# Rotary attention loop of a four-layer kernel: from sixteen steps of 128 queries to eight key chunks of 256 queries

## The chip, the cores and the metric

The kernel runs on one core of a Trainium2 chip, as one program. The time is the device time of one execution in microseconds (us). A core has these engines: PE (TensorE, matrix multiplies; its weight loads are listed apart as PEld), DVE (VectorE), ACT (ScalarE), POOL (GpSimd) and SP (SyncE, which here only issues DMAs). Each engine runs its own instructions in order and waits on semaphores that others raise. Matrix results land in PSUM, which has eight banks of 128 x 512 fp32; everything else is in SBUF.

## The reference

The input `x` is 8 images of 32 x 32 tokens with 192 channels, fp32. Four layers follow one another, each of the form `x = x + layer(_gn(x))` with a group normalisation without weights. Layers 0 and 2 are attention with relative positions, layer 1 is windowed attention with registers. Layer 3, which the change touches, is this, cut to what matters (12 heads of 16 channels):

```python
q = x @ wq.T + bq;  k = (x @ wk.T + bk) * scaling;  v = x @ wv.T + bv
qr = theta_shift(qh, sin, cos);  kr = theta_shift(kh, sin, cos)    # rotary
qk = einsum('bnld,bnmd->bnlm', qr, kr) + mask                      # mask: (12, 1024, 1024)
out = einsum('bnlm,bnmd->bnld', softmax(qk, axis=-1), vr)
return (out + lepe(v)) @ wo.T + bo
```

For each image and head there are 1024 x 1024 scores, a full mask of the same size is added, and the softmax runs over the 1024 keys.

## The kernel before, in words

`program` runs the layers in turn. For layer 3, `prepare_rot` writes the rotated queries and keys and the values to DRAM, and `attend_rot` does the attention. All of the change is in `attend_rot`.

`attend_rot` works through 96 units: 3 groups of 4 heads, times 4 quarters of the queries (256 each), times 8 images. A unit has 256 queries, seen as two blocks of 128 (index `c`), 4 heads (`G`; in two pairs `p`, two sides `sd`), and 1024 keys in 8 chunks of 128 (`kc`). One unit goes through these stages:

- `scores` (PE, L2413), four calls per unit, one for each (c, p): four matmuls of 512 columns fill `S`, which takes four PSUM banks and is one buffer. A call therefore waits (`s_done`) until DVE has read the result of the call before.
- `row_max` (DVE): for each of the two heads of a call a pass (L2498) adds the mask, writes the sum to `X` in SBUF and keeps the row maximum. Then DVE subtracts the maximum for one of the two heads (L2503, "scalar" below), and ACT does so for the other (`lower`, L2550). They raise `x_dve` and `x_act`.
- `transposed` (PE, L2426): four 128 x 128 transposes of `X` fill one bank of `T`. `T` is a ring of three banks, taken in the order of `ORDER`: the transposes, and the two steps of the tail. `free` makes each wait for the reader of what stood three places before.
- `exponential` (ACT, L2531): the exponential of one bank of `T`, 128 x 512, into `PROB`, a ring of four in SBUF.
- `outputs` (PE, L2438): values times `PROB`, accumulated in `O` over the key chunks. The four heads are four column strips of 32. It has eight matmul instructions (two per head, as the trace counts them) of 128 columns.
- The tail of a unit runs inside the next one: ACT copies `O` to `OSB` (L2539); PE spreads the softmax sums (`turn`, L2449, two matmuls of 256 columns); DVE takes the reciprocal (L2509) and multiplies (L2511), together `divide`; PE projects (`wo`, L2454, four matmuls of 256 columns); ACT copies to `Y` (L2544); POOL adds it to the output in DRAM.

The order of PE's work is written out by hand. `body(u)` has 16 steps; step s is block c = s // 8, chunk kc = s % 8. A step does `transposed(s)`, a `scores` call of the next unit in chunks 1 and 5 of either block, `outputs(s - 1)`, and after steps 3 and 6 the tail's `turn` and `wo`. The transposes of block 0 wait for the four rows of block 0 alone, those of block 1 for block 1. ACT's order is written beside it: the exponentials, `lower` after steps 1, 5, 9 and 13 (that of the pair (1, 1) in step 1 of the unit that uses it), the two copies after steps 0 and 6. DVE does `row_max(0, 0)`, `divide`, `row_max(0, 1)`, `(1, 0)`, `(1, 1)`. PE and ACT run two units per turn of a hardware loop (`Fori`). Before each group of PE instructions stands `alone(pe)`, a nop that carries the waits.

Of the kernel before, what the change touches and what calls it, by code (L numbers as in the profile page):

```python
# [42 lines left out]
def need(eng, sem, value, solo=False):  # L43

    if isinstance(value, int) and value <= 0:
        return
    eng.wait_ge(sem, value)
    if solo:
        alone(eng)
# [2190 lines left out]
def attend_rot(nc, sems, name, stream, w, ident, part_rows, v_rows):  # L2240

    QUARTERS = GROUPS * 4
    UNITS = QUARTERS * IMAGES
    RING, PRING = 3, 4
    STEPS = 2 * CHUNKS
    SCORES_AT = {1: 0, 5: 1}
    TAIL = ("turn", "wo")
    TAIL_AT = {3: "turn", 6: "wo"}
    ORDER = [n for s in range(STEPS) for n in [("t", s)] + ([TAIL_AT[s]] if s in TAIL_AT else [])]
    assert len(ORDER) % RING == 0  # L2250

    def kind(n):
# [10 lines left out]
    def slot(n):  # L2263
        return ORDER.index(n) % RING

    with ExitStack() as ctx:
        def sb(n, shape, dt=F32):
            return ctx.enter_context(nc.sbuf_tensor(f"{name}_{n}", shape, dt))
# [12 lines left out]
        K = sb("K", [P, 2, 2, TOKENS], F32R)  # L2281
        QR = sb("QR", [P, 2, 2, 2 * P], F32R)
        V = sb("V", [P, 2, CHUNKS, G, 2 * DIM])
        PROB = sb("PROB", [P, PRING, G, P])
        OSB = sb("OSB", [P, 2 * P])
        inverse = sb("inverse", [P, 2 * P])
        Y = sb("Y", [HALF, 2, 2, 2 * P])
# [102 lines left out]
        def _(pe):  # L2390
# [24 lines left out]
                        if kh:  # L2415
                            last.then_inc(s_ready, 1)

            def transposed(u, par, s):
                c, kc = divmod(s, CHUNKS)
                free(u, ("t", s))  # L2420
                if kc == 0:
                    pe.wait_ge(x_dve, G * u + 2 * (c + 1))
                    pe.wait_ge(x_act, G * u + 2 * (c + 1))
                alone(pe)
                for g in range(G):
                    last = nc.tensor.transpose(T[:, slot(("t", s)), P * g:P * g + P], X[:, par, c, g, P * kc:P * kc + P],  # L2426
                                               ident_sb[:])
                last.then_inc(t_ready, 1)

            def outputs(u, par, s, mine=None):  # L2430
                c, kc = divmod(s, CHUNKS)
                pe.wait_ge(t_act, upto(u, ("t", s), "act"))
                if s == 0:
                    pe.wait_ge(v_loaded[par], V_LOADS * mine)
                    need(pe, o_out, u)
                alone(pe)
                for g in range(G):
                    last = nc.tensor.matmul(O[Q * g:Q * g + Q, par, P * c:P * c + P], V[:, par, kc, g],  # L2438
                                            PROB[:, s % PRING, g], start=kc == 0, stop=kc == CHUNKS - 1)
                last.then_inc(pv_done, 1)  # L2440

            def tail(u, par, n):
# [20 lines left out]

            def body(u, par, mine, nth):

                for s in range(STEPS):
                    c, kc = divmod(s, CHUNKS)
                    transposed(u, par, s)
                    if kc in SCORES_AT and not (isinstance(u, int) and u == UNITS - 1):
                        scores(u + 1, 1 - par, c, SCORES_AT[kc], nth)  # L2470
                    if s:
                        outputs(u, par, s - 1, mine)
                    elif not isinstance(u, int) or u:
                        outputs(u - 1, 1 - par, STEPS - 1)
                    if s in TAIL_AT and (not isinstance(u, int) or u):
                        tail(u, par, TAIL_AT[s])

            def epilogue():
                outputs(UNITS - 1, 1, STEPS - 1)
                for n in TAIL:  # L2480
                    tail(UNITS, 0, n)

# [4 lines left out]
        def _(eng):  # L2487
# [26 lines left out]
                for p in range(2):  # L2514
                    row_max(0, c, p)
            for u in range(UNITS + 1):
                for c in range(2):
                    if u + 1 < UNITS:
                        row_max(u + 1, c, 0)
                    if c == 0 and u:  # L2520
                        divide(u - 1)
                    if u + 1 < UNITS:
                        row_max(u + 1, c, 1)


        @block.scalar
        def _(act):
            def exponential(u, s):
                act.wait_ge(t_ready, upto(u, ("t", s), "pe"))
                need(act, pv_done, STEPS * u + s - PRING + 1, solo=True)  # L2530
                nc.scalar.activation(PROB[:, s % PRING].rearrange("p g x -> p (g x)"), T[:, slot(("t", s))], ACT.Exp,  # L2531
                                     scale=-1.0).then_inc(t_act, 1)

            def outputs(u, opar):
                act.wait_ge(pv_done, STEPS * u)
                if not isinstance(u, int) or u > 1:
                    act.wait_ge(t_ready, upto(u - 1, "wo", "pe"))
                alone(act)
                nc.scalar.copy(OSB[:], O[:, opar]).then_inc(o_out, 1)  # L2539

            def projected(u, ypar, stores):
                act.wait_ge(t_ready, upto(u, "wo", "pe"))
                need(act, y_stored[ypar], 16 * stores, solo=True)
                nc.scalar.copy(Y[:, ypar].rearrange("p m t -> p (m t)"), T[0:HALF, slot("wo")]).then_inc(t_act, 1)  # L2544

            def lower(v, par, c, p):

                act.wait_ge(s_done, TILES_U * v + G * c + 2 * p + 2)
                here = X[:, par, c, 2 * p + 1]
                nc.scalar.activation(here, here, ACT.Identity, scale=-1.0, bias=rmax[:, par, c, 2 * p + 1:2 * p + 2]  # L2550
                                     ).then_inc(x_act, 1)

            def body(u, par, stores):
                last = isinstance(u, int) and u == UNITS - 1
                for s in range(STEPS):
                    exponential(u, s)
                    c, kc = divmod(s, CHUNKS)
                    if kc == 1 and c == 0:
                        lower(u, par, 1, 1)
                    elif kc == 1 and not last:  # L2560
                        lower(u + 1, 1 - par, 0, 1)
                    if kc == 5 and not last:
                        lower(u + 1, 1 - par, c, 0)
                    if not isinstance(u, int) or u:
                        if s == 0:
                            outputs(u, 1 - par)
                        if s == 6:
                            projected(u, 1 - par, stores)

            for c, p in ((0, 0), (0, 1), (1, 0)):  # L2570
                lower(0, 0, c, p)
            for u in range(4):
                body(u, u % 2, (u - 1) // 2)
            with act.Fori(2, UNITS // 2 - 1) as p:
                body(2 * p, 0, p - 1)
                body(2 * p + 1, 1, p)
            body(UNITS - 2, 0, UNITS // 2 - 2)
            body(UNITS - 1, 1, UNITS // 2 - 1)
            outputs(UNITS, 1)
            projected(UNITS, 1, UNITS // 2 - 1)  # L2580

# [137 lines left out]
```

## Time and profile before

| what | value |
|---|---|
| time, median of 3 runs | 9231.04 us (9228.94 to 9237.27) |
| time of the profiled execution | 9223.04 us |
| its span, first to last instruction | 9221.4 us |
| the loop of `attend_rot`, first to last exponential | 7320.5 to 9208.5 us of the span |
| PE busy over the span | 7542.9 us (82%) |
| DVE, ACT, POOL busy | 57%, 49%, 28% |
| granted PE clock, mean | 0.900 of full speed |

The span is measured from the first to the last instruction of the profiled execution; the 1.6 us around it are start and end. A busy share is an average over four layers with different limits, so the rows further down are of stretches of the rotary loop. A granted clock of 1.00 is 2.4 GHz and 0.50 is 1.2 GHz. A timeline row gives when a run of like instructions starts, how long it takes from its first start to its last end, and in brackets how long the engine had been idle and what ended that.

### The profile page before, as it was taken

The numbers are of one execution on the slowest core, as the hardware profiler recorded it, in microseconds if no ns is written. First come the engines' busy times: TensorE is split into PE (matmuls) and PEld (weight loads), VectorE is DVE, ScalarE is ACT, GpSimd is POOL, SyncE is SP. The second block draws the span as 40 slices with busy tenths as digits, with TensorE's granted clock in tenths as the row PEclk, the third lists the DMA queues.
The fourth block names the chain that finished last, engine by engine and source line by source line (L and its number), as shares of the span: only waits on it lengthen the run. The fifth ranks groups of instructions, "written<-read, shape, count | busy, mean of one in ns | idle before, by whom it ended". The sixth has DMA issues, their size and how long they took to land. (4 is left out here: it accounts for less than half of the span.)

```text
span 9221.4 us, 201937 instructions
## 1 busy us (share of the span) xinstructions
PE 7542.9 (82%) x68440; PEld 4564.9 (50%) x68440; DVE 5284.4 (57%) x7803; ACT 4527.8 (49%) x8209; POOL 2587.1 (28%) x2843
## 2 busy tenths in 40 slices
PE   2988889889388878846889888888576699999999
PEld 2555555555155555524555555554232355555555
DVE  3555555555255555544555555554677477777776
ACT  1444444444265655632444444445233377777776
POOL 2343434333021121114433333342455300000000
PEclk7899999999698999977999998999677799999999
DMA  6666666665433333346665665664221344444443
GB/s 160 130 119 135 122 130 118 130 123 105 112 70 68 75 70 71 74 118 126 126 128 120 122 126 118 123 117 74 92 72 62 88 123 112 126 111 123 115 122 82
DMA packets 536710, 999.89 MB, mean 108 GB/s; under 512 B 102129, under 2 KB 303026, under 8 KB 500210
## 3 DMA queue, kind: packets, MB, share of 16 engines
q1 hardware_dynamic: 479346, 900.57, 43.6%
q0 software_dynamic: 56576, 88.90, 6.2%
q8 instruction: 485, 7.95, 0.4%
q14 instruction: 303, 2.48, 0.1%
HBM read 646.02 MB, written 335.81 MB: 106 GB/s over the span
## 5 line engine op out<-in xcount | busy, mean ns | idle before, releaser
L1676 DVE TENSOR_REDUCE a_nmp<-a_S 128x2 f32<-128x1024 f32 x1536 | 1878.3, 1224 | 1433.6 <-PE a_S L1524 1430.5
L1777 ACT ACTIVATE a_PROB<-a_T 128x512 f32<-128x512 f32 x3072 | 1667.3, 595 | 1977.5 <-PE a_T L1503 1964.2
L1373 POOL CAST a_RF<-a_RL 32x512 fp32r<-32x512 f32 x1536 | 1295.2, 843 | 1011.8 <-DVE a_RL L1704 919.9
L2498 DVE CUSTOM_DVE_ANT_0 a_X<-a_S,a_mask 128x1024 f32<-128x1024 f32 x768 | 909.3, 1221 | 608.7 <-PE a_S L2413 593.4
L2531 ACT ACTIVATE a_PROB<-a_T 128x512 f32<-128x512 f32 x1536 | 918.2, 598 | 439.1 <-PE a_T L2426 429.3
L1499 PE MATMUL a_T<-a_QW,a_KW 64*128 64x512 f32 x3072 | 801.1, 514 | 402.0 <-issue 149.1
L2426 PE MATMUL a_T<-a_ident,a_X 128*128 128x128 f32 x6144 | 994.6, 285 | 32.2 <-DVE a_OSB L2511 16.5
L1499 PEld LDWEIGHTS a_T<-a_QW,a_KW 64*128 64x128 f32 x3072 | 311.3, 191 | 1427.1 <-issue 1424.2
L1537 PE MATMUL a_O<-a_PROB,a_V 128*32 128x512 f32 x6144 | 887.8, 652 | 2.9 <-ACT a_PROB L1777 2.5
L962 DVE CUSTOM_DVE_ANT_0 a_PROB<-a_S,a_mask 128x512 f32<-128x512 f32 x768 | 522.9, 688 | 598.5 <-PE a_PT L799 505.8
L2426 PEld LDWEIGHTS a_T<-a_ident,a_X 128*128 128x128 f32 x6144 | 660.0, 141 | 327.1 <-issue 305.5
L1524 PEld LDWEIGHTS a_S<-a_KV,a_QV 64*128 64x128 f32 x6144 | 652.1, 199 | 116.8
L1518 PE MATMUL a_S<-a_KW,a_QW 64*128 64x512 f32 x3072 | 662.8, 418 | 27.3 <-DVE a_nmp L1676 27.3
L1503 PE MATMUL a_T<-a_QV,a_KV 64*128 64x512 f32 x3072 | 648.0, 409 | 35.1 <-issue 35.1
L1524 PE MATMUL a_S<-a_KV,a_QV 64*128 64x256 f32 x6144 | 660.9, 290 | 0.0
L2438 PE MATMUL a_O<-a_PROB,a_V 128*32 128x128 f32 x12288 | 655.0, 284 | 2.0 <-ACT a_PROB L2531 0.5
L2369 POOL DMA_DIRECT2D out<-a_Y x96 | 92.0, 959 | 1845.6 <-ACT a_PROB L2531 1832.5
L1043 ACT ACTIVATE a_PROB<-a_PROB,a_nmax 128x512 f32<-128x512 f32 x768 | 550.4, 719 | 76.1 <-DVE a_nmax L962 76.1
L1564 PE MATMUL a_T<-a_QC,a_tab_d 16*32 16x64 f32 x6144 | 414.3, 300 | 181.9 <-issue 106.0
L799 PE MATMUL a_PT<-a_ident,a_PROB 128*128 128x128 f32 x3072 | 491.8, 285 | 50.4 <-ACT a_PROB L1043 31.0
L1564 PEld LDWEIGHTS a_T<-a_QC,a_tab_d 16*32 16x32 f32 x6144 | 362.8, 127 | 207.8 <-issue 186.5
L2550 ACT ACTIVATE a_X<-a_X,a_rmax 128x1024 f32<-128x1024 f32 x384 | 438.6, 1142 | 38.0 <-DVE a_rmax L2498 38.0
(160 smaller groups left out, 10640.8 us busy)
## 6 DMA issues: line engine op xcount, KB each, us to landing
a_QV<-a_part_rows SPq DMA_DIRECT2D x384, 256.0 KB, 7.1
a_rel_rows<-a_RF SPq DMA_DIRECT2D x96, 1024.0 KB, 9.2
a_K<-part_rows SPq DMA_DIRECT2D x576, 128.0 KB, 3.3
a_X<-xn_scratch SPq DMA_DIRECT2D x72, 768.0 KB, 6.4
stream<-a_Y POOLq DMA_DIRECT2D x288, 192.0 KB, 5.7
a_part_rows<-a_part SPq DMA_DIRECT2D x48, 1024.0 KB, 11.8
a_QV<-a_part_rows SPq DMA_DIRECT2D x384, 128.0 KB, 7.7
a_QV<-a_rel_rows SPq DMA_DIRECT2D x384, 128.0 KB, 7.4
```

Of the source, the lines that this page charges most:

```text
L1373: nc.gpsimd.tensor_copy(dst, src).then_inc(permuted, 1)
L1499: nc.tensor.matmul(T[:, slot(("st", s, pr, sd))], KW[lines, keys], QW[lines, par, pr, cols], start=True, stop=False)
L1518: nc.tensor.matmul(S[:, pr, sd], QW[lines, par, pr, queries], KW[lines, kh * BANK:(kh + 1) * BANK], start=True, stop=False)
L1524: last = nc.tensor.matmul(S[:, pr, sd, here], QV[lines, par, pr, 2 * kh + kq, queries], KV[lines, par, pr, keys], start=False, stop=kq == 1)
L1537: last = nc.tensor.matmul(O[Q * g:Q * g + Q], V[:, par, kc, g], PROB[:, s % PRING, g], start=kc == 0, stop=kc == CHUNKS - 1)
L1564: last = nc.tensor.matmul(T[at + 32:at + 64, to, 64 * a:64 * a + 64], tab_d[:, x], QC[:, :, half * BANK + x:(half + 1) * BANK:SIDE], start ...
L1676: nc.vector.tensor_reduce(nmp[:, qh, c, 2 * pr:2 * pr + 2, kh], S[:, pr], AX.X, ALU.max).then_inc(s_done, 1)
L1777: nc.scalar.activation(PROB[:, s % PRING, 2 * pr + sd], T[:, slot(("st", s, pr, sd))], ACT.Exp).then_inc(t_act, 1)
L2426: last = nc.tensor.transpose(T[:, slot(("t", s)), P * g:P * g + P], X[:, par, c, g, P * kc:P * kc + P], ident_sb[:])
L2438: last = nc.tensor.matmul(O[Q * g:Q * g + Q, par, P * c:P * c + P], V[:, par, kc, g], PROB[:, s % PRING, g], start=kc == 0, stop=kc == CHU ...
L2498: nc.vector.tensor_tensor_reduce(out=X[:, v % 2, c, g], in0=S[:, sd].rearrange("p a b -> p (a b)"), in1=mask[:, n % 2, g, c], scale=1.0, s ...
L2531: nc.scalar.activation(PROB[:, s % PRING].rearrange("p g x -> p (g x)"), T[:, slot(("t", s))], ACT.Exp, scale=-1.0).then_inc(t_act, 1)
```

## The change: steps over key chunks

The unit keeps its 256 queries, 4 heads and 8 key chunks. `body` now has 8 steps, one for each key chunk.

- In a step PE fills two banks of `T` one after the other: `transposed(kc, 0)` has the heads of pair 0 for both query blocks, `transposed(kc, 1)` those of pair 1. There are 16 such calls per unit as before, of four transposes each. The first of a unit waits for all eight rows of the unit (both blocks and pairs) where it waited for four.
- ACT takes the exponential of each bank; the two fill one entry of `PROB`, which is twice as wide (256 queries). The ring has three entries and not four.
- `outputs` runs once per key chunk, 8 times per unit and not 16, with eight matmul instructions of 256 columns each.
- The four `scores` calls of the next unit stand in steps 0, 2, 3 and 5. In sixteenths of the unit they stood at 1, 5, 9 and 13; now they stand at 0, 4, 6 and 10.
- The tail: `turn` after step 1, `wo` after step 4 (sixteenths 2 and 8; they stood at 3 and 6).
- ACT's `lower` calls for the next unit stand in steps 2, 4, 5 and 7. The last, for the pair (1, 1), stands behind the last exponential of the unit; it stood in the second step of the unit that uses it. The prologue lowers four pairs and not three.
- DVE's order of calls is the same. SP's and POOL's programs are not touched.

The diff, with PE's `body` and `tail` order, ACT and DVE:

```diff
@@ -2241,12 +2241,12 @@
 
     QUARTERS = GROUPS * 4
     UNITS = QUARTERS * IMAGES
-    RING, PRING = 3, 4
-    STEPS = 2 * CHUNKS
-    SCORES_AT = {1: 0, 5: 1}
+    RING, PRING = 3, 3
+    SCORES_AT = {0: (0, 0), 2: (0, 1), 3: (1, 0), 5: (1, 1)}
     TAIL = ("turn", "wo")
-    TAIL_AT = {3: "turn", 6: "wo"}
-    ORDER = [n for s in range(STEPS) for n in [("t", s)] + ([TAIL_AT[s]] if s in TAIL_AT else [])]
+    TAIL_AT = {1: "turn", 4: "wo"}
+    LOWER_AT = {2: (0, 0), 4: (0, 1), 5: (1, 0), 7: (1, 1)}
+    ORDER = [n for s in range(CHUNKS) for n in [("t", s, 0), ("t", s, 1)] + ([TAIL_AT[s]] if s in TAIL_AT else [])]
     assert len(ORDER) % RING == 0
 
     def kind(n):
@@ -2281,7 +2281,7 @@
         K = sb("K", [P, 2, 2, TOKENS], F32R)
         QR = sb("QR", [P, 2, 2, 2 * P], F32R)
         V = sb("V", [P, 2, CHUNKS, G, 2 * DIM])
-        PROB = sb("PROB", [P, PRING, G, P])
+        PROB = sb("PROB", [P, PRING, G, 2 * P])
         OSB = sb("OSB", [P, 2 * P])
         inverse = sb("inverse", [P, 2 * P])
         Y = sb("Y", [HALF, 2, 2, 2 * P])
@@ -2415,28 +2415,27 @@
                         if kh:
                             last.then_inc(s_ready, 1)
 
-            def transposed(u, par, s):
-                c, kc = divmod(s, CHUNKS)
-                free(u, ("t", s))
+            def transposed(u, par, kc, p):
+                free(u, ("t", kc, p))
+                if kc == 0 and p == 0:
+                    pe.wait_ge(x_dve, G * (u + 1))
+                    pe.wait_ge(x_act, G * (u + 1))
+                alone(pe)
+                for sd in range(2):
+                    for c in range(2):
+                        last = nc.tensor.transpose(T[:, slot(("t", kc, p)), P * (2 * sd + c):P * (2 * sd + c) + P],
+                                                   X[:, par, c, 2 * p + sd, P * kc:P * kc + P], ident_sb[:])
+                last.then_inc(t_ready, 1)
+
+            def outputs(u, par, kc, mine=None):
+                pe.wait_ge(t_act, upto(u, ("t", kc, 1), "act"))
                 if kc == 0:
-                    pe.wait_ge(x_dve, G * u + 2 * (c + 1))
-                    pe.wait_ge(x_act, G * u + 2 * (c + 1))
-                alone(pe)
-                for g in range(G):
-                    last = nc.tensor.transpose(T[:, slot(("t", s)), P * g:P * g + P], X[:, par, c, g, P * kc:P * kc + P],
-                                               ident_sb[:])
-                last.then_inc(t_ready, 1)
-
-            def outputs(u, par, s, mine=None):
-                c, kc = divmod(s, CHUNKS)
-                pe.wait_ge(t_act, upto(u, ("t", s), "act"))
-                if s == 0:
                     pe.wait_ge(v_loaded[par], V_LOADS * mine)
                     need(pe, o_out, u)
                 alone(pe)
                 for g in range(G):
-                    last = nc.tensor.matmul(O[Q * g:Q * g + Q, par, P * c:P * c + P], V[:, par, kc, g],
-                                            PROB[:, s % PRING, g], start=kc == 0, stop=kc == CHUNKS - 1)
+                    last = nc.tensor.matmul(O[Q * g:Q * g + Q, par], V[:, par, kc, g], PROB[:, kc % PRING, g],
+                                            start=kc == 0, stop=kc == CHUNKS - 1)
                 last.then_inc(pv_done, 1)
 
             def tail(u, par, n):
@@ -2463,20 +2462,20 @@
 
             def body(u, par, mine, nth):
 
-                for s in range(STEPS):
-                    c, kc = divmod(s, CHUNKS)
-                    transposed(u, par, s)
+                for kc in range(CHUNKS):
+                    for p in range(2):
+                        transposed(u, par, kc, p)
                     if kc in SCORES_AT and not (isinstance(u, int) and u == UNITS - 1):
-                        scores(u + 1, 1 - par, c, SCORES_AT[kc], nth)
-                    if s:
-                        outputs(u, par, s - 1, mine)
+                        scores(u + 1, 1 - par, *SCORES_AT[kc], nth)
+                    if kc:
+                        outputs(u, par, kc - 1, mine)
                     elif not isinstance(u, int) or u:
-                        outputs(u - 1, 1 - par, STEPS - 1)
-                    if s in TAIL_AT and (not isinstance(u, int) or u):
-                        tail(u, par, TAIL_AT[s])
+                        outputs(u - 1, 1 - par, CHUNKS - 1)
+                    if kc in TAIL_AT and (not isinstance(u, int) or u):
+                        tail(u, par, TAIL_AT[kc])
 
             def epilogue():
-                outputs(UNITS - 1, 1, STEPS - 1)
+                outputs(UNITS - 1, 1, CHUNKS - 1)
                 for n in TAIL:
                     tail(UNITS, 0, n)
 
@@ -2514,25 +2513,27 @@
                 for p in range(2):
                     row_max(0, c, p)
             for u in range(UNITS + 1):
-                for c in range(2):
-                    if u + 1 < UNITS:
-                        row_max(u + 1, c, 0)
-                    if c == 0 and u:
-                        divide(u - 1)
-                    if u + 1 < UNITS:
-                        row_max(u + 1, c, 1)
+                if u + 1 < UNITS:
+                    row_max(u + 1, 0, 0)
+                if u:
+                    divide(u - 1)
+                if u + 1 < UNITS:
+                    row_max(u + 1, 0, 1)
+                    row_max(u + 1, 1, 0)
+                    row_max(u + 1, 1, 1)
 
 
         @block.scalar
         def _(act):
-            def exponential(u, s):
-                act.wait_ge(t_ready, upto(u, ("t", s), "pe"))
-                need(act, pv_done, STEPS * u + s - PRING + 1, solo=True)
-                nc.scalar.activation(PROB[:, s % PRING].rearrange("p g x -> p (g x)"), T[:, slot(("t", s))], ACT.Exp,
-                                     scale=-1.0).then_inc(t_act, 1)
+            def exponential(u, kc, p):
+                act.wait_ge(t_ready, upto(u, ("t", kc, p), "pe"))
+                if p == 0:
+                    need(act, pv_done, CHUNKS * u + kc - PRING + 1, solo=True)
+                nc.scalar.activation(PROB[:, kc % PRING, 2 * p:2 * p + 2].rearrange("p g x -> p (g x)"),
+                                     T[:, slot(("t", kc, p))], ACT.Exp, scale=-1.0).then_inc(t_act, 1)
 
             def outputs(u, opar):
-                act.wait_ge(pv_done, STEPS * u)
+                act.wait_ge(pv_done, CHUNKS * u)
                 if not isinstance(u, int) or u > 1:
                     act.wait_ge(t_ready, upto(u - 1, "wo", "pe"))
                 alone(act)
@@ -2552,22 +2553,18 @@
 
             def body(u, par, stores):
                 last = isinstance(u, int) and u == UNITS - 1
-                for s in range(STEPS):
-                    exponential(u, s)
-                    c, kc = divmod(s, CHUNKS)
-                    if kc == 1 and c == 0:
-                        lower(u, par, 1, 1)
-                    elif kc == 1 and not last:
-                        lower(u + 1, 1 - par, 0, 1)
-                    if kc == 5 and not last:
-                        lower(u + 1, 1 - par, c, 0)
-                    if not isinstance(u, int) or u:
-                        if s == 0:
-                            outputs(u, 1 - par)
-                        if s == 6:
-                            projected(u, 1 - par, stores)
-
-            for c, p in ((0, 0), (0, 1), (1, 0)):
+                later = not isinstance(u, int) or u
+                for kc in range(CHUNKS):
+                    exponential(u, kc, 0)
+                    exponential(u, kc, 1)
+                    if kc == 0 and later:
+                        outputs(u, 1 - par)
+                    if kc in LOWER_AT and not last:
+                        lower(u + 1, 1 - par, *LOWER_AT[kc])
+                    if kc == 4 and later:
+                        projected(u, 1 - par, stores)
+
+            for c, p in ((0, 0), (0, 1), (1, 0), (1, 1)):
                 lower(0, 0, c, p)
             for u in range(4):
                 body(u, u % 2, (u - 1) // 2)
```

## Rows read from the trace of the kernel before

**Rows 1.** Busy time in 300 us of the loop: PE, PEld, DVE, ACT, POOL, clock, DMA.
```profile
7700.00:8000.00 300.00, 294.15 (x3252) 175.78 (x3245) 216.68 (x335) 218.36 (x334) 14.38 (x15) 1.00 0.43 115
```

**Rows 2.** DMA issues from 7700 to 8900 us: count, KB each, median us to landing.
```profile
a_V<-v_rows SPq DMA_DIRECT2D x61, 512.0 KB, 4.2
```

**Rows 3.** The tile a_PROB, its exponentials: shortest/median/longest ns, first and last start.
```profile
L2531 ACT ACTIVATE a_PROB<-a_T x1536: 588/597/602, 7320.5 to 9208.5; 128x512 f32<-128x512 f32 x192
```

**Rows 4.** Timeline of PE: start, length, line, operation, count, idle before.
```profile
8029.62 0.63 PE L2426 MATMUL a_T<-a_ident,a_X 128*128 128x128 f32 x4 [0.29 <-issue]
...
8034.06 0.70 PE L2449 MATMUL a_T<-a_OSB,a_turn 128*128 128x256 f32 x2
8034.60 0.60 PE L2426 MATMUL a_T<-a_ident,a_X 128*128 128x128 f32 x4
8035.13 0.43 PE L2438 MATMUL a_O<-a_PROB,a_V 128*32 128x128 f32 x8
8035.48 0.66 PE L2426 MATMUL a_T<-a_ident,a_X 128*128 128x128 f32 x4
8036.07 0.73 PE L2413 MATMUL a_S<-a_K,a_QR 48*128 48x512 f32 x4
8036.73 0.42 PE L2438 MATMUL a_O<-a_PROB,a_V 128*32 128x128 f32 x8
8037.34 0.63 PE L2426 MATMUL a_T<-a_ident,a_X 128*128 128x128 f32 x4 [0.18 <-DVE a_OSB L2511]
...
8038.25 1.10 PE L2454 MATMUL a_T<-a_OSB,a_wo 128*96 128x256 f32 x4
8039.19 0.60 PE L2426 MATMUL a_T<-a_ident,a_X 128*128 128x128 f32 x4
8039.73 0.42 PE L2438 MATMUL a_O<-a_PROB,a_V 128*32 128x128 f32 x8
```

**Rows 5.** Timeline in layer 0: an output group of 512 columns and what follows.
```profile
2008.89 1.07 PE L1537 MATMUL a_O<-a_PROB,a_V 128*32 128x512 f32 x8
...
2009.89 0.50 PE L1499 MATMUL a_T<-a_QW,a_KW 64*128 64x512 f32 x2
```

**Rows 6.** Timeline of all engines in one unit of the loop.
```profile
8006.21 0.42 PEld L2426 LDWEIGHTS a_T<-a_ident,a_X 128*128 128x128 f32 x4 [0.20 <-issue]
...
8006.80 0.73 PE L2413 MATMUL a_S<-a_K,a_QR 48*128 48x512 f32 x4
8007.04 0.60 ACT L2531 ACTIVATE a_PROB<-a_T 128x512 f32<-128x512 f32 x1 [0.34 <-PE a_T L2426]
...
8007.53 1.14 ACT L2550 ACTIVATE a_X<-a_X,a_rmax 128x1024 f32<-128x1024 f32 x1
...
8007.70 1.23 DVE L2498 CUSTOM_DVE_ANT_0 a_X<-a_S,a_mask 128x1024 f32<-128x1024 f32 x1 [1.43 <-PE a_S L2413]
...
8014.47 0.75 DVE L2503 TENSOR_SCALAR a_X<-a_X,a_rmax 128x1024 f32<-128x1024 f32 x1
...
8015.13 1.75 DVE L2509 RECIPROCAL a_inverse<-a_T 128x256 f32<-128x256 f32 x1
...
8016.92 0.42 DVE L2511 TENSOR_TENSOR a_OSB<-a_OSB,a_inverse 128x256 f32<-128x256 f32 x1
...
8017.26 1.22 DVE L2498 CUSTOM_DVE_ANT_0 a_X<-a_S,a_mask 128x1024 f32<-128x1024 f32 x1
8017.46 0.42 PEld L2426 LDWEIGHTS a_T<-a_ident,a_X 128*128 128x128 f32 x4 [0.42 <-issue]
```

**Rows 7.** Timeline of the prologue, where `scores` has nothing else to wait for.
```profile
7307.93 1.23 DVE L2498 CUSTOM_DVE_ANT_0 a_X<-a_S,a_mask 128x1024 f32<-128x1024 f32 x1 [84.78 <-PE a_S L2413]
...
7310.22 0.75 DVE L2503 TENSOR_SCALAR a_X<-a_X,a_rmax 128x1024 f32<-128x1024 f32 x1
...
7310.42 0.53 PEld L2413 LDWEIGHTS a_S<-a_K,a_QR 48*128 48x128 f32 x4 [3.32 <-issue]
```

**Rows 8.** Busy time in a stretch of layer 1, columns as in Rows 1.
```profile
3900.00:4000.00 100.00, 84.26 (x937) 56.84 (x930) 64.03 (x167) 69.75 (x171) 16.04 (x22) 0.95 0.30 58
```

## The prediction, made before the changed kernel ran

> **What bounds the kernel now.** I read the busy time of a stretch first. In the loop PE is busy 294 of 300 us at a granted clock of 1.00 (2.4 GHz), while DVE and ACT have 217 and 218 [rows 1]. So the loop ends when PE's list of instructions ends, and the other two follow. The brackets of the timeline say the same: ACT sits idle 0.34 us until the transposes are there, DVE 1.43 us until the scores are there [rows 6]. The exponentials of units 0 to 95 start between 7320.5 and 9208.5 us, so a unit takes 1888 / 95.94 = 19.68 us [rows 3]. In the timeline of PE the reader is to see start-to-start times: transposes to scores 0.59, output group to transposes 0.35, scores to output group 0.66 [rows 4].
>
> From these a unit of before is 16 x (0.59 + 0.36) + 4 x 0.66, plus 0.48 for `turn` and 0.90 for `wo`, which is 19.2 us. Two small waits come on top. The transposes after step 5 start 0.61 us after the output group instead of 0.36, because DVE's multiply holds their bank: 0.25 us. The loop branch costs 0.36 us in every second unit, so 0.18 (0.29 us of idle in its row). Sum 19.6 us, against 19.68 measured. This method is then good to 0.1 us per unit, and I use it for the new order.
>
> **The change part by part: PE's work.**
>
> Output groups. At 128 columns a group takes 0.36 us until the next starts [rows 4], at 512 columns 1.00 us [rows 5]. On a straight line 256 columns take 0.36 + 0.64 / 3 = 0.573 us. The eight of them are 4.58 us, where sixteen took 5.76. The ends of the range are 0.50 (half of the 512 group) and 0.66.
>
> Pairs of transposes. Two groups in a row with nothing between are not in the trace. The nearest rows are `turn` followed by transposes. From a `turn` of the same 0.43 us of columns to the transposes is 0.54 us, and from these to the output group 0.53 [rows 4]. I take 0.535 + 0.54 = 1.075 us for a pair, against 2 x 0.59 = 1.18 apart. The ends are 0.86 + 0.11 (no gap at all between the two) and 1.18.
>
> The work of a new unit is 8 x 1.075 + 8 x 0.573 + 4 x 0.66 + 0.48 + 0.90 = 17.2 us, 2.0 us less than before. If nothing else changed, a unit would take 17.2 to 17.3 us.
>
> **The waits that it adds.** The steps are now bunched, so I lay out one unit by start times on PE, from its first transposes at 0. These pieces are measured:
> - scores to DVE's first pass 0.90 (8006.80 to 8007.70); transposes to exponential 0.83 (8006.21 to 8007.04); an exponential followed by ACT's next instruction 0.49 (8007.04 to 8007.53); `lower` 1.14 long [rows 6];
> - DVE: scalar to reciprocal 0.66, reciprocal to multiply 1.79, multiply to next pass 0.34; the end of the multiply (8017.34) to PE's start 0.12 [rows 6];
> - first pass to scalar 2.29, and first pass to the next `scores` call, when that waits for DVE, 2.49 [rows 7].
>
> First wait, the single score buffer. The scores (0,0) start at 1.075, DVE's passes at 1.98, the scalar at 4.27. PE goes on: scores 0.66 and outputs 0.573 (2.31), a pair and outputs (3.96), `turn`, ready some 0.9 later. So DVE takes the reciprocal at 4.93, the multiply at 6.72, and the passes for (0,1) only at 7.06. The scores (1,0) can then start at 7.06 + 2.49 = 9.55. Meanwhile PE has `turn` (to 4.43), a pair (5.51), scores (0,1) (6.17) and outputs (6.74). The next transposes take the bank of `turn`, which is free at 6.72 + 0.42 + 0.12 = 7.26: 0.52 us of wait. Their pair ends at 8.34, and the scores (1,0), one chunk behind (0,1), wait 1.21 us. Before, a `scores` call came every four of sixteen steps, some 4.5 us apart, which covers DVE's 3.4 us; now (0,1) and (1,0) are 2.3 us apart in PE's order and DVE has `divide` in front. Everything of PE queues behind that call, and ACT runs dry with it.
>
> Second wait, the end of the unit. From 9.55: scores and outputs (10.78); chunk 4 with `wo` 2.55 (13.33); chunk 5 with scores 2.31 (15.64); chunk 6 1.65 (17.29). The last pair starts at 17.29. Its first exponential starts at 18.12, its second at 18.61, and only then comes `lower` (1,1), from 19.10 to 20.24. The next unit's first transposes need it: 20.24 + 0.12 = 20.36. PE had its last outputs of this unit done at 18.94, so it waits 1.42 us. The branch of 0.36 us lies inside this wait. Before, that same `lower` ran in step 1 and was needed in step 8. DVE's own part of these rows is done before (scores at 14.41, scalar at 17.6), so the wait is ACT's order and not its load.
>
> Sum of a unit: 17.2 + 0.52 + 1.21 + 1.42 = 20.36 us. That is 0.68 us more than 19.68: the 2.0 us of work and 0.43 of small waits come back, 3.15 of waits are added.
>
> **Parts at nothing.** `PROB` with three entries: the exponential of chunk kc needs the outputs of kc - 3, two chunks back in PE's order; if that cover went, ACT would wait, which has about a third of its time free. The copies to `OSB` and `Y`: ACT idles until the next exponential. SP: the load of V is issued after `wo`, now at about 13.4 of 20.4 us, and is needed at 3.4 of the next unit, so it has 10 us; it lands in 4.2 [rows 2]. The operands are loaded more than a unit ahead, as before. POOL only stores, a unit behind.
>
> **The ends.** Unit 0 waits for all four pairs of rows, some 4 us more than now (the first pass of the fourth pair plus 2.4 for DVE and 1.3 for `lower`). But it has no tail and no `divide` in its chain, which makes it about 1 us shorter than before, and the last unit has no scores: 8 x 1.65 = 13.2 against 16 x 0.95 = 15.2. Together about +1 us.
>
> 94 units x 0.68 + 1 = 65 us. The profiled execution of 9223 us (span 9221.4) becomes 9288. The median of the runs shown is 8 us above it, so I predict 9296 us.
>
> **A rule of the skill on the clock.** During the loop, where about half of PE's time is transposes, the granted clock is 1.00 [rows 1]. The Trainium skill, page "TensorE: Matmul & The Clock Gate", section "Part 4: PE-mode transpose", says that the full clock "doesn't engage" for transposes, as they do not count as busy in the same way. The trace does not agree as long as PE has no gaps. The changed loop has gaps, with pairs of transposes on both sides of them; that is the second rival.
>
> **The rivals.**
> - Cheap pairs: the second group of transposes streams right behind the first, and the output group is at its low end, 0.50. For it: after `turn` and `wo` the transposes' weights are loaded early (their own length is 0.60 and not 0.66) [rows 4]. Against: 0.54 us from `turn` to transposes is already 0.11 above bare streaming. With pairs at 0.97 and groups at 0.50 the same layout, laid out anew, gives 19.65 us per unit, as now: 9229. With cheap pairs alone it gives 19.94: 9231 + 94 x 0.26 + 1 = 9256. Chance 0.15, of which 0.09 for what lies within 18 us of before.
> - The clock falls: for a stretch after the gaps of 1.2 and 1.4 us PE runs at 1.2 GHz. For it: in layer 1, with PE busy 84 of 100 us, the mean clock is 0.95 [rows 8], and the changed loop has 17.2 / 20.36 = 84%. Against: 0.95 is still mostly full clock, and the instructions there are others. A mean of 0.95 is a tenth of the time at half clock, 2 us of each unit, in which half of the work comes late: 1.0 us per unit, 9296 + 94 = 9390. Chance 0.13.
> - No waits: DVE and ACT hand over in time and PE's work alone counts, 17.3 us per unit: 9231 - 94 x 2.4 = 9005. It would need the reciprocal and `lower` to be off the chain, and the rows put them on it. Chance 0.04.
>
> The other side decides at one point: when the sum of the three waits is under 2.4 us per unit, the change is faster.
>
> **How the numbers follow.** The forecast itself has 0.68; its own range, with pairs of 1.00 to 1.18 (20.1 to 20.8 us per unit), is 9268 to 9345. A measurement of this kernel can tell 0.2% (18 us) from no change. Faster by more than that is the no-wait case and the far end of the cheap pairs: 0.06. The same is their middle: 0.09. Slower is the rest: 0.85. For the range I go down to 9245, inside the cheap pairs, and up to 9385, almost the whole of the clock case.
>
> **What would show it.** In the trace after: output groups of 256 columns 0.57 us before their successor; the second transposes 0.54 us after the first; two idle times of PE per unit, over 1 us each, one before L2413 released by DVE L2498 in every unit, one before L2426 released by ACT L2550; a third of 0.5 us before L2426 released by DVE L2511; PE busy about 84% in the loop, clock 1.00; exponentials of a unit 20.4 us apart. The prediction is wrong if either long wait is missing, if pairs take under 1.0 us, or if the clock in the loop is under 0.98.

## The result: 0.8% slower, as forecast, by a sum whose parts were each somewhat off

The changed kernel takes 9297.48 us (median of 5 runs), the kernel before 9231.04. The ratio is 1.0077, 95% interval 1.0056 to 1.0098. The forecast was 9296. In a later set of four executions of the same changed kernel one took 20728 us at a mean granted clock of 0.57; it is left out of that set's ratio.

The profiled execution took 9314.65 us, 92 more than that of before. Not all of it is the change. The layers ahead are the same code and end a little earlier or later from run to run: the first `scores` call starts at 7306.61 us before and at 7321.68 after, and at 7300.57 in another profile of the same changed kernel. From that call to the last instruction it is 1914.8 us before and 1990.9 after. The change costs 76 us there; the medians of all runs differ by 66.

The busy time of the loop, the row that answers to [rows 1], with the same columns:

```profile
7700.00:8000.00 300.00, 253.57 (x2213) 154.95 (x2212) 205.31 (x320) 201.55 (x325) 14.39 (x15) 0.98 0.49 118
```

PE is busy 254 of 300 us (85%) where it had 294, and the granted clock is 0.98 where it was 1.00. No engine is full any more. The exponentials, which answer to [rows 3]:

```profile
L2532 ACT ACTIVATE a_PROB<-a_T x1536: 591/596/621, 7339.4 to 9298.9; 128x512 f32<-128x512 f32 x192
```

(9298.9 - 7339.4) / 95.94 = 20.42 us per unit; the forecast had 20.36, before it was 19.68. Now one unit on PE, the rows that answer to [rows 4]:

```profile
8014.73 1.07 PE L2426 MATMUL a_T<-a_ident,a_X 128*128 128x128 f32 x8 [1.39 <-issue]
8015.73 0.73 PE L2413 MATMUL a_S<-a_K,a_QR 48*128 48x512 f32 x4
8016.39 0.64 PE L2437 MATMUL a_O<-a_PROB,a_V 128*32 128x256 f32 x8
8016.96 1.09 PE L2426 MATMUL a_T<-a_ident,a_X 128*128 128x128 f32 x8
8017.98 0.64 PE L2437 MATMUL a_O<-a_PROB,a_V 128*32 128x256 f32 x8
8018.55 0.70 PE L2448 MATMUL a_T<-a_OSB,a_turn 128*128 128x256 f32 x2
8019.09 1.04 PE L2426 MATMUL a_T<-a_ident,a_X 128*128 128x128 f32 x8
8020.05 0.73 PE L2413 MATMUL a_S<-a_K,a_QR 48*128 48x512 f32 x4
8020.72 0.64 PE L2437 MATMUL a_O<-a_PROB,a_V 128*32 128x256 f32 x8
8021.95 1.06 PE L2426 MATMUL a_T<-a_ident,a_X 128*128 128x128 f32 x8 [0.59 <-DVE a_OSB L2510]
8024.23 0.73 PE L2413 MATMUL a_S<-a_K,a_QR 48*128 48x512 f32 x4 [1.22 <-DVE a_rmax L2497]
...
8032.81 0.64 PE L2437 MATMUL a_O<-a_PROB,a_V 128*32 128x256 f32 x8
8034.83 1.06 PE L2426 MATMUL a_T<-a_ident,a_X 128*128 128x128 f32 x8 [1.38 <-issue]
```

The reader is to see four things. The two groups of transposes of a step are now one run of eight and take 1.00 to 1.03 us to what follows, 0.96 behind `turn`. The output group takes 0.57. There are three idle times: 0.59 for the bank of `turn`, 1.22 in front of the scores (1, 0), and 1.4 in front of the next unit's first transposes. And the unit is 20.10 us long (8034.83 - 8014.73).

What ends the idle time of 1.4 us is shown as "issue"; the timeline of all engines at that place shows who holds PE back:

```profile
8012.51 1.08 ACT L2532 ACTIVATE a_PROB<-a_T 128x512 f32<-128x512 f32 x2 [0.50 <-PE a_T L2426]
...
8013.48 1.15 ACT L2551 ACTIVATE a_X<-a_X,a_rmax 128x1024 f32<-128x1024 f32 x1
8014.70 0.86 PEld L2426 LDWEIGHTS a_T<-a_ident,a_X 128*128 128x128 f32 x8 [1.84 <-issue]
```

Two exponentials, then `lower`, which ends at 14.63, and 0.07 us later PE loads weights. From 7700 to 8900 us these waits come once per unit (59 units; total, times, longest):

```profile
PE a_T L2426 <- issue: 81.7, 59, 1.4
PE a_S L2413 <- DVE a_rmax L2497: 70.9, 58, 1.2
...
PE a_T L2426 <- DVE a_OSB L2510: 34.4, 58, 0.9
```

The mean of a unit, 20.42 us, is above 20.10 because not all are alike. From reciprocal to reciprocal mostly three units take 20.1 us and the fourth 21.6 (23 such units in the loop). This is PE in a long one:

```profile
8042.05 1.06 PE L2426 MATMUL a_T<-a_ident,a_X 128*128 128x128 f32 x8 [0.59 <-DVE a_OSB L2510]
8044.33 1.04 PE L2413 MATMUL a_S<-a_K,a_QR 48*128 48x512 f32 x4 [1.22 <-DVE a_rmax L2497]
8045.31 1.08 PE L2437 MATMUL a_O<-a_PROB,a_V 128*32 128x256 f32 x8
8046.32 1.88 PE L2426 MATMUL a_T<-a_ident,a_X 128*128 128x128 f32 x8
8048.13 0.64 PE L2437 MATMUL a_O<-a_PROB,a_V 128*32 128x256 f32 x8
```

The busy time of 4 us around the same place, with the columns of [rows 1]:

```profile
8044.00:8048.00 4.00, 3.67 (x20) 2.12 (x20) 3.36 (x8) 0.40 (x1) 0.00 (x0) 0.57 0.01 2
```

Behind the idle times of 0.59 and 1.22 us the scores take 1.04 and not 0.73, the output group 1.08 and not 0.64, the transposes 1.88 and not 1.09. The granted clock of these 4 us is 0.57, so most of them ran at half clock (1.2 GHz); at 8048.13 all is at full length again. Such a stretch is called a dip from here on. From the scores to the output group at 8048.13 PE takes 3.80 us, where the unit before took 2.26 (8024.23 to 8026.49), and nothing behind takes the 1.54 us up: the unit is 1.55 us longer. 23 dips are 36 us. The remaining 40 us are 94 x (20.10 - 19.68); in that the prologue, 3.8 us longer, is about offset by the first and last units, which are shorter.

### The profile page after: what moved, and what is told of

It reads as the page before. It is cut to its first block and busy times, and to the rows that moved or that the text cites. A ratio compares the mean times of both kernels' runs of the same rounds, so it can differ in the third digit from the quotient of the medians.

```text
span 9312.6 us, 187162 instructions
## 1 busy us (share of the span) xinstructions
PE 7337.7 (79%) x62296; PEld 4460.8 (48%) x62296; DVE 5284.9 (57%) x7803; ACT 4460.1 (48%) x8209; POOL 2594.5 (28%) x2843
## 5 line engine op out<-in xcount | busy, mean ns | idle before, releaser
L1777 ACT ACTIVATE a_PROB<-a_T 128x512 f32<-128x512 f32 x3072 | 1667.9, 595 | 1962.4 <-PE a_T L1503 1949.5
L2532 ACT ACTIVATE a_PROB<-a_T 128x512 f32<-128x512 f32 x1536 | 835.8, 595 | 596.3 <-PE a_T L2426 589.3
L2426 PE MATMUL a_T<-a_ident,a_X 128*128 128x128 f32 x6144 | 842.4, 281 | 192.2 <-issue 127.2
L2426 PEld LDWEIGHTS a_T<-a_ident,a_X 128*128 128x128 f32 x6144 | 690.4, 144 | 470.0 <-issue 448.1
L2437 PE MATMUL a_O<-a_PROB,a_V 128*32 128x256 f32 x6144 | 501.4, 399 | 0.3 <-ACT a_PROB L2532 0.3
```

What stands on the lines that cost most here:

```text
L1777: nc.scalar.activation(PROB[:, s % PRING, 2 * pr + sd], T[:, slot(("st", s, pr, sd))], ACT.Exp).then_inc(t_act, 1)
L2426: last = nc.tensor.transpose(T[:, slot(("t", kc, p)), P * (2 * sd + c):P * (2 * sd + c) + P], X[:, par, c, 2 * p + sd, P * kc:P * kc + P], ...
L2437: last = nc.tensor.matmul(O[Q * g:Q * g + Q, par], V[:, par, kc, g], PROB[:, kc % PRING, g], start=kc == 0, stop=kc == CHUNKS - 1)
L2532: nc.scalar.activation(PROB[:, kc % PRING, 2 * p:2 * p + 2].rearrange("p g x -> p (g x)"), T[:, slot(("t", kc, p))], ACT.Exp, scale=-1.0). ...
```

## The experiments

Four kernels first, to see whether the two long waits are separate terms.

**Lowering of (1, 1) one step earlier.**

```diff
-    LOWER_AT = {2: (0, 0), 4: (0, 1), 5: (1, 0), 7: (1, 1)}
+    LOWER_AT = {2: (0, 0), 4: (0, 1), 5: (1, 0), 6: (1, 1)}
```

> The changed kernel with one edit: ACT lowers the pair (1, 1) after step 6 and not after step 7, so that it is done before the last exponentials of the unit. Theory A (the two long waits are separate terms, the one at the unit's end is ACT's order alone): the wait before the first transposes of a unit, 1.4 us, goes to about nothing; the loop branch of 0.36 us in every second unit shows again; the wait before the scores (1, 0) stays at 1.2. Undisturbed units of 18.8 and 19.2 us in turn instead of 20.10, time about 9190 with the clock's dips as they are. Theory B (the end wait only hides DVE's chain, the scores and row maxima are the real bound): the wait moves in front of a scores call and the unit stays within 0.2 us of 20.1. Theory C on the clock: the dips come at the scores wait, which stays, so the granted clock in the loop stays at 0.98 or so; if they need the end wait as well, it is 1.00.

Measured: 9257.65 us, ratio to before 1.0042 (1.0026 to 1.0057). The wait at the unit's end is gone, and a unit without a dip takes 18.89 us. But of the 95 steps from reciprocal to reciprocal only 18 are of that kind; 75 take 20.4 us or a little more. The busy time of 1200 us, with the clock of 0.93:

```profile
7700.00:8900.00 1200.00, 1087.46 (x8956) 653.57 (x8951) 845.82 (x1313) 816.75 (x1314) 57.31 (x60) 0.93 0.49 118
```

and PE around one dip, in a run of units of 20.45 us:

```profile
8014.86 1.06 PE L2426 MATMUL a_T<-a_ident,a_X 128*128 128x128 f32 x8 [0.59 <-DVE a_OSB L2510]
8017.15 0.73 PE L2413 MATMUL a_S<-a_K,a_QR 48*128 48x512 f32 x4 [1.22 <-DVE a_rmax L2497]
8017.81 1.08 PE L2437 MATMUL a_O<-a_PROB,a_V 128*32 128x256 f32 x8
8018.82 1.97 PE L2426 MATMUL a_T<-a_ident,a_X 128*128 128x128 f32 x8
```

The mechanism of theory A holds (18.89 against 18.8 and 19.2), theory B falls. The expectation of 9190 us missed by 68: the clock took back most of the 1.2 us per unit. Theory C expected a clock of 0.98 or 1.00, and it is 0.93. The units of 18.8 and 19.2 us in turn did not come either: the loop branch, 0.36 us in every second unit before the change, shows in none of the changed kernels whose wait at the unit's end is gone. Why is open.

**Scores (1, 0) in step 4.**

```diff
-    SCORES_AT = {0: (0, 0), 2: (0, 1), 3: (1, 0), 5: (1, 1)}
+    SCORES_AT = {0: (0, 0), 2: (0, 1), 4: (1, 0), 5: (1, 1)}
```

> The changed kernel with one edit: the scores (1, 0) are issued in step 4 and not in step 3. Theory A (single score buffer with the divide in DVE's chain): the wait of 1.2 us before scores (1, 0) goes, the 0.6 us before the transposes of step 3 stays, the wait at the unit's end stays at 1.4 us; units of 19.1 us instead of 20.10, time about 9200 before any effect of the clock. Theory B (DVE's chain is the bound): DVE's work only comes later, the unit's end waits longer by as much, and the unit stays at 20.1. Clock: with no wait over 0.6 us in mid-unit the dips in every fourth unit go and the clock in the loop is 1.00, which is worth another 0.39 us per unit, 37 us: 9165.

Measured: 9181.81 us, ratio 0.9956 (0.9940 to 0.9972). Units of 19.10 us throughout, no dips:

```profile
PE a_T L2426 <- issue: 87.2, 63, 1.4
...
PE a_T L2426 <- DVE a_OSB L2510: 37.3, 63, 0.9
...
PE a_S L2413 <- DVE a_rmax L2497: 13.6, 62, 0.2
```

The wait in front of the scores went from 1.2 to 0.2 us, and the one at the unit's end stayed at 1.4. So one digit in this table turns the change from slower into 0.4% faster. With idle times of 1.4, 0.6 and 0.2 us, each several us from the next, there is no dip here. The time is 17 us above the 9165 that was expected with the clock at 1.00.

**Both edits.**

> Both edits: scores (1, 0) in step 4, lowering of (1, 1) after step 6. Theory A: the gains add up, since each wait is a term of its own: units of 17.8 and 18.1 us in turn (PE's work of 16.9 us, 0.6 of wait for the divide, small waits, the branch), clock 1.00, time about 9055; faster than the kernel before the change by some 1.9%. Theory B: the second edit gains less than alone, because DVE's chain of four scores calls and one divide (4 x 3.4 + 2.1 = 15.7 us) is met; units over 18.5.

Measured: 9043.8 us, ratio 0.9813 (0.9792 to 0.9835), units of 17.86 us, clock 1.00. The two gains add up: 20.10 - 1.21 - 1.00 = 17.89. Theory B falls.

**Scores first.** Against the changed kernel, the call for (0, 0) moves ahead of the transposes of step 0, (1, 0) stands in step 4 as in the run before, and three lowerings come one step earlier:

```diff
-    SCORES_AT = {0: (0, 0), 2: (0, 1), 3: (1, 0), 5: (1, 1)}
-    LOWER_AT = {2: (0, 0), 4: (0, 1), 5: (1, 0), 7: (1, 1)}
+    SCORES_AT = {2: (0, 1), 4: (1, 0), 5: (1, 1)}
+    LOWER_AT = {1: (0, 0), 3: (0, 1), 5: (1, 0), 6: (1, 1)}
...
                 for kc in range(CHUNKS):
+                    if kc == 0 and not (isinstance(u, int) and u == UNITS - 1):
+                        scores(u + 1, 1 - par, 0, 0, nth)
                     for p in range(2):
                         transposed(u, par, kc, p)
```

> Scores (0, 0) of the next unit stand ahead of the first transposes, the others in steps 2, 4 and 5; lowering after steps 1, 3, 5 and 6. DVE starts its chain 1 us earlier in the unit. Theory A: the divide is then done before the transposes of step 3 want its bank, or nearly, and units take 17.5 and 17.8 us in turn, which is PE's work and the branch: time about 9030. Theory B: the scores call ahead of the transposes delays the first exponentials by 0.66 us and ACT's list becomes the bound; units above e3's.

Measured: 9008.1 us, ratio 0.9774 (0.9757 to 0.9790). Units of 17.38 us, PE busy 97% again:

```profile
7700.00:8000.00 300.00, 291.20 (x2590) 178.80 (x2589) 246.32 (x382) 232.72 (x379) 16.30 (x17) 1.00 0.55 134
```

This is the best version of the study, 2.3% faster than the kernel before the change. Theory B fell: the units are shorter than the 17.86 us of the kernel with both edits, and ACT is busy 233 of 300 us.

**Evenly spread scores.** The eight-chunk structure without the early scores:

```diff
-    SCORES_AT = {0: (0, 0), 2: (0, 1), 3: (1, 0), 5: (1, 1)}
+    SCORES_AT = {0: (0, 0), 2: (0, 1), 4: (1, 0), 6: (1, 1)}
```

> The changed kernel with the four scores calls evenly spread, in steps 0, 2, 4 and 6, as they were in sixteenths before; `lower` as in the change. So this is the eight-chunk structure without the early scores. Theory A (the early scores buy nothing, they cost): no wait in front of any scores call over 0.3 us, but the last one is later; ACT's order at the unit's end still costs 1.4 us; units of 19.1 us, clock 1.00, time within 15 us of the kernel with only scores (1, 0) moved (9182). Rival (the call in step 6 makes the row maximum of (1, 1) late for the unit's end): the chain scores 0.9, DVE 2.4, lower 1.3 from step 6 ends after ACT's last exponentials, and units are 19.6 or more.

Measured: 9209.4 us, ratio 0.9983 (0.9967 to 1.0000). Undisturbed units are 19.10 us, as expected. The wait at the unit's end is 1.67 us and follows ACT directly:

```profile
7761.18 1.06 PE L2426 MATMUL a_T<-a_ident,a_X 128*128 128x128 f32 x8 [1.67 <-ACT a_X L2551]
```

The time missed its expectation: it is 27 us above 9182, where 15 were allowed, because 29 of 95 units take 20.3 or 20.4 us, with a mean clock of 0.97 from 7700 to 8900 us. Behind the idle time of 1.67 us above, the transposes at 7763.72 us take 1.97 us where 1.09 is their length at full clock; the idle time before that, for the bank of `turn`, lies some 12 us earlier. So one idle time of 1.67 us can do what 1.4 did not. Why it does so in some units only, no run here shows.

**What brings the clock down.** Three kernels with useless work, all on the kernel with `lower` after step 6, where dips were most frequent. The transposes of step 3, pair 1, are issued three times:

```diff
             def transposed(u, par, kc, p):
...
                 alone(pe)
+                if (kc, p) == (3, 1):
+                    for _ in range(2):
+                        for sd in range(2):
+                            for c in range(2):
+                                nc.tensor.transpose(T[:, slot(("t", kc, p)), P * (2 * sd + c):P * (2 * sd + c) + P],
+                                                    X[:, par, c, 2 * p + sd, P * kc:P * kc + P], ident_sb[:])
```

> The kernel with `lower` (1, 1) after step 6, plus useless work: the four transposes of step 3, pair 1, are issued three times and not once (eight more transposes, 0.85 us), ahead of the wait for scores (1, 0). They lie inside that wait, so no chain gets longer. Theory C (the granted clock falls because PE is idle 0.6 and then 1.2 us of 2.9 us around that call): with 0.4 us of idle time left there the clock is 1.00, all units take 18.9 us where five of seven took 20.4, and the time falls by 94 x 1.1 = 100 us, to about 9155, although work was added. Rival D (transposes do not count for the clock, as the Trainium skill has it on its page TensorE: Matmul & The Clock Gate, Part 4): the dips stay, time about 9258. Rival E (the dips have another cause): the same.

In the second, ordinary matmuls stand in their place:

```diff
+                if (kc, p) == (3, 1):
+                    for sd in range(2):
+                        nc.tensor.matmul(T[:, slot(("t", kc, p)), 2 * P * sd:2 * P * sd + 2 * P], ident_sb[:],
+                                         X[:, par, sd, 2 * p, P * kc:P * kc + 2 * P], start=True, stop=True)
```

> As the run before, but the useless work is four ordinary fp32 matmul instructions of 256 columns (0.85 us) in front of the transposes of step 3, pair 1, written to the bank that these overwrite. Theory C: clock 1.00, units of 18.9 us, 9155. If D holds and transposes do not count but matmuls do, this one gets the clock back and the run before does not. Rival E: dips in both, 9258.

In the third, the condition is `(kc, p) == (2, 1)` and the transposes are issued twice:

> The kernel with `lower` (1, 1) after step 6, plus the transposes of step 2, pair 1, issued twice (0.43 us more), ahead of the wait of 0.6 us for the bank of `turn`. The wait of 1.2 us before scores (1, 0) stays. If both idle times together bring the clock down, dips become fewer or go: clock above 0.97, time 9160 to 9210. If the wait of 1.2 us is enough alone: clock 0.93 to 0.94, time about 9258.

Measured: 9152.17, 9151.44 and 9150.66 us, ratios 0.9926, 0.9918 and 0.9928 (lowest bound 0.9894, highest 0.9958). All three have units of 18.89 us throughout and a clock of 1.00; without the useless work it is 9257.65 us (ratio 1.0042). The undisturbed unit is the same 18.89 us with and without it, so the whole gain is the clock's. In the first, the idle times are 0.59 and 0.35 us, with 1.9 us of work between (8007.87 to 8009.81). The clock and the waits of the third, where only the first idle time was filled:

```profile
7700.00:8000.00 300.00, 276.39 (x2444) 170.93 (x2436) 225.24 (x350) 216.97 (x350) 15.34 (x16) 1.00 0.51 122
...
PE a_S L2413 <- DVE a_rmax L2503: 78.3, 64, 1.2
PE a_T L2432 <- DVE a_OSB L2516: 7.9, 48, 0.5
```

The wait of 1.2 us is still in every unit and does not bring the clock down alone. What did it was 0.59 and 1.22 us of idle time with one pair of transposes between. Filling either is enough. Rival D falls: transposes held the clock up as matmuls did. The Trainium skill, page "TensorE: Matmul & The Clock Gate", section "Part 4: PE-mode transpose", has it that transposes do not count as busy in the same way and that the full clock does not engage for them. These runs do not agree: 9152.17 us with transposes and 9151.44 with matmuls. Rival E falls with it.

**The changed kernel with the same fill, and the changed kernel again.** The first has the edit of the run with fill by transposes, on the changed kernel:

> The changed kernel itself with the useless transposes of step 3, pair 1 (issued three times), inside the wait for scores (1, 0). Theory C: the dips in every fourth unit go, all units take 20.10 us, clock in the loop 1.00; against the changed kernel 24 dips of 1.55 us fall away, 37 us, so the ratio to the kernel before is 1.0077 - 0.0040 = 1.0037 and the time some 9255. What then remains, 94 x (20.10 - 19.68) = 39 us, is the net of the change at full clock. Rival: the wait of 1.4 us at the unit's end keeps the dips, time unchanged at about 9290.

> The changed kernel as it is, on the same chip and beside the same runs of the kernel before as the run with fill. Every theory: ratio within 1.0056 to 1.0098, units of 20.1 us with one of 21.6 in every four, first exponential some microseconds earlier or later than in the profile before, as the layers ahead vary.

Measured, beside the same runs of before (median 9231.55 us): 9272.44 us, ratio 1.0040 (1.0027 to 1.0054), with the fill; ratio 1.0075 (1.0056 to 1.0095) without. With the fill the loop has units of 20.10 us throughout and this row:

```profile
8000.00:8300.00 300.00, 265.22 (x2361) 167.27 (x2361) 212.03 (x330) 204.56 (x329) 14.37 (x15) 1.00 0.49 118
```

The wait of 1.4 us at the unit's end is still there (83.0 us in 60 units), so it does not keep the dips. Of the 0.75 to 0.77% of the change, 0.40% is what the added waits cost beyond the saved work, at full clock, and some 0.35% is the clock.

## Why the prediction was right, step by step

- **PE's list bounds the loop before.** Right; where the waits are taken out, PE is 97% busy again (291 of 300 us) and the gain of the structure appears.
- **Output groups, 0.573 us.** Right: 0.57 from start to start (8006.38 to 8006.95 in the same profile). The straight line between 128 and 512 columns holds.
- **Pairs of transposes, 1.075 us.** Too high, and this was the largest error of the sum. They take 1.00 to 1.03 us, and 0.96 or 0.97 behind `turn` and `wo`. Together with the tail PE spends 9.5 us per unit on them, where the forecast had 9.98. The second group streams right behind the first. The lower end of the stated bounds (0.97) was nearer than the value taken. The work of a unit is 16.7 us and not 17.2.
- **First waits, 0.52 and 1.21 us.** Right in place and order. Against undisturbed start-to-start times (0.57 and 1.00) they are 0.66 and 1.28. PE came earlier, since its pairs were shorter, but DVE did not: the scores (1, 0) start 9.50 us into the unit (8014.73 to 8024.23), where the layout had 9.55.
- **Wait at the unit's end, 1.42 us.** Right: 1.45, and behind `lower` as forecast. The kernel with `lower` a step earlier loses it and 1.21 us per unit with it.
- **The sum of a unit, 20.36.** 16.7 + 3.4 = 20.10 at full clock. The excess of work (0.49) and the shortfall of the waits (0.25) partly cancelled: an error in PE's part in front of a wait for DVE is taken up by the wait. Behind the scores (1, 0) there is no such wait, and from there to the unit's end it is 10.60 us where the layout had 10.81.
- **The clock, a rival with chance 0.13.** It came, at a smaller size than priced: a mean of 0.98 and not 0.95, 0.39 us per unit and not 1.0. That 9296 lies so close to the measured time is luck: the clock, which the forecast's sum held at full speed, and the cheaper pairs cancel. By the forecast's own mechanism alone, with pairs as they were, the time would have been 9231 + 94 x 0.42 + 1 = 9271, and the run with fill measured 1.0040, which is 9268 for a kernel of 9231. That is slower too, but at the lowest end of the 9268 to 9345 that the prediction gives for its mechanism. The direction and the waits are earned, the last 25 us are not.
- **The line "clock under 0.98 in the loop" as a sign of error** was only just not met (0.98), and the sign "pairs under 1.0 us" was met by the two of eight pairs that stand behind `turn` and `wo`. Both point at the two terms that were off.
- **Parts at nothing.** Right: no wait on the load of V or on SP is among PE's waits in the loop. ACT waits there 357.2 us for the transposes and 34.7 us in front of the copy to `OSB`, and no wait for an entry of `PROB` is among its waits.
- **The loop branch.** The prediction places its 0.36 us inside the wait at the unit's end. Where that wait is gone it does not appear, so this part of the account is not borne out; it changed nothing in the sum.
- **The ends.** The prologue is longer as forecast: from the first scores to the first exponential 7321.68 to 7339.37, 17.7 us, against 13.9 before; the forecast had some 4 us more.

## What to carry to other kernels

A hand-written order should be laid out against the slowest hand-over of a single buffer: here scores, 0.9 us to DVE, 2.4 us of DVE, and whatever DVE does in between. Two calls closer together than that stall everything behind them. When a change merges two halves into one, look at what each half waited for: the merged start waits for the last of both, and the work that made it ready in mid-unit now stands at the end. In this kernel two short idle times close together took the clock down, which cost up to 1.5 us per unit on top of their length, and the cure was to move one of them, or even to fill it.

## What the runs showed of the hardware that was not expected

- Idle times of PE of 0.59 and 1.22 us with 1.0 us of work between brought the granted clock to 1.2 GHz (mean of 0.57 from 8044 to 8048 us in the profile after): in one unit of four with undisturbed units of 20.10 us, in 75 of 95 with undisturbed units of 18.89. An idle time of 1.4 us, with 0.6 and 0.2 elsewhere in the unit, did not do so in units of 19.10 us; one of 1.2 us behind a remainder of 0.16 did not at 18.89; one of 1.67 us did in 29 of 95 units. Why some units are hit and others not is open.
- 0.43 us of useless transposes made a kernel 107 us faster (9257.65 to 9150.66; against the kernel before, 1.0042 to 0.9928), 1.1 us in each of 96 units.
- Transposes keep the clock up as well as fp32 matmuls of the same length: 9152.17 against 9151.44 us.
- A group of four 128 x 128 transposes behind another takes about 0.43 us (1.02 - 0.59; in the run with the first idle time filled, 0.44 from start to start), where one behind an output group takes 0.59 to the next group.
